# Output projections of four query tiles as two pairs, each in one PSUM bank with one sum of 512 columns, in the second and third slot of an attention round

## Chip, cores and metric

One core of a Trainium2 chip runs the whole program in one launch. The metric is the device time in microseconds (us), lower is better. In the profile PE is TensorE's matmuls, PEld its weight loads, DVE is VectorE, ACT is ScalarE, POOL is GpSimd and SP is SyncE.

## The reference

A layer norm is followed by attention and by a mixture of experts, whose result gates the attention's:

```python
xn = _layernorm(x, axis=-1)                       # x: (4, 512, 256)
q, k, v = xn @ Wq, xn @ Wk, xn @ Wv               # 16 query heads, 4 key/value heads of 128
q, k = rope_xpos(q), rope_xpos(k)
attn = softmax(where(causal, q @ k.T / sqrt(128), -inf))
s = (attn @ v).reshape(B, S, 2048) @ Wo           # the output projection: 2048 -> 256
g = _silu(moe(xn))                                # 16 experts, top 2, and a shared one
out = x + s * g
```

## The kernel before

Attention runs in 16 **rounds**. Round i handles group i: one batch of 512 tokens and one key/value head with its four query heads (j = 0 to 3). Every value of importance is kept as a pair of a high and a low half (fp16 and bf16), so each product is three matmuls (`PASSES`).

Five engines work on a round at the same time, each with its instructions in an order written out by hand (`round_`, once for each engine), and they meet only through semaphores that count upwards. For head h the stages are:

- TensorE `score` (L1465): scores of a head, three PSUM banks, 1280 columns in all.
- VectorE `row_max` (L1151) masks and takes the maximum; ScalarE `exponentials` (L809); VectorE `invert_sums` (L1157) gives 1/sum; GpSimd `divide` (L569) multiplies the probabilities by it.
- TensorE `transpose_probs` (L1478): ten transposes of the divided probabilities, in three units (0, 1) and (2); ScalarE copies the high half (L817), VectorE subtracts the low half (L1163).
- TensorE `weigh_values` (L1494): probabilities times values into bank 5; ScalarE `output_hi` (L831), VectorE `output_lo` (L1169).
- TensorE `project_out(rd, q)` (L1510): in round i the finished heads of round i - 1 are multiplied by Wo for query tile q, 4 heads x 3 passes = 12 matmuls of 256 columns; VectorE `add_projection` (L1176) adds the result to `s_sb` in SBUF.

In the same round the queries and the key of round i + 1 are prepared: TensorE `project` (L1434) of q0, q1, k, q2, q3, VectorE `rotate_products` (L1133, L1137, L1138), GpSimd `rotate_sum` (L556), ScalarE `rotate_hi` (L797), GpSimd `rotate_lo` (L563). Projections of all kinds are **items**: they use PSUM banks 6 and 7 in turn, in the order of a list. The item at place n waits until the item at place n - 2 has been read (`misc_free`). `project_values` (L1449, L1142) is the item v.

TensorE's order in a round of the loop, with `score(0')` for head 0 of the next round (T is `transpose_probs`, W is `weigh_values`):

| slot | order on TensorE |
|---|---|
| j = 0 | score(1), q0, T(0; 0, 1), W(last head of the round before), v, T(0; 2) |
| j = 1 | score(2), T(1; 0, 1), q1, **o0**, T(1; 2), W(0) |
| j = 2 | score(3), T(2; 0, 1), k, **o1**, T(2; 2), W(1) |
| end | q2, **o2**, T(3; 0, 1), W(2), score(0'), q3, T(3; 2), **o3** |

VectorE's order at the end of a round is `output_lo(1)`, the products of q2, `add_projection(2)`, the low halves of T(3; 0, 1), `row_max` of head 0', `output_lo(2)`, the first product of q3, `invert_sums` of head 0', the other products of q3, the low half of T(3; 2), `add_projection(3)`. GpSimd's is `divide` of head 3, the sum of k, the low halves of q1 and k, the sum of q2, an extra part (`ahead_of_division`), `divide` of head 0', the low half of q2.

The extra part differs between rounds. Rounds 6 to 13 scatter the rows of two token tiles to DRAM there and in the slots before (L598, L602); rounds 1 to 5 prepare weights and the routing of tokens to experts on GpSimd and VectorE; round 14 prepares shared weights (L587). Rounds 7 to 13 are a hardware loop, the others are unrolled. In round 0 there is no earlier output to project. Round 15 prepares no next round. After it, in the epilogue, o0 to o3 of the last group follow one another on TensorE, and then the expert part begins.

Of the kernel before, what the change touches and what calls it, by code (L numbers as in the profile page):

```python
# [18 lines left out]
P = 128  # L19
B, S, D = 4, 512, 256  # L20
# [54 lines left out]
ITEMS_FIRST = ["q0", "v", "x10", "q1", "x11", "x20", "k", "x21", "x30", "q2", "q3", "x31"]  # L75
ITEMS_LOGITS = ["q0", "v", "g0", "q1", "o0", "g1", "k", "o1", "g2", "q2", "o2", "q3", "o3", "g3"]
ITEMS_RANK = ["q0", "v", "rank", "q1", "o0", "k", "o1", "q2", "o2", "q3", "o3"]
ITEMS_TILE = ["q0", "v", "q1", "o0", "k", "o1", "q2", "o2", "q3", "o3", "tile"]
ITEMS_LOOP = ["q0", "v", "q1", "o0", "k", "o1", "q2", "o2", "q3", "o3"]
ITEMS_LAST = ["v", "o0", "o1", "o2", "o3"]  # L80
ITEMS_EPILOGUE = ["o0", "o1", "o2", "o3"]

# [120 lines left out]
def build(nc, x, wq, wk, wv, wo, gate_t, w_gate_up, w_down, shared_gu, shared_down, rope, ident, mask, iota, tri, rows, digits, out):  # L203
    with ExitStack() as ctx:
# [16 lines left out]
        s_sb = sb("s_sb", [P, NT * D], F32)  # L221
# [765 lines left out]
        def _(dve):  # L987
# [183 lines left out]

            def add_projection(rd, q):
                at = ((rd.i - 1) // NKV) * (QT * D) + q * D
                dve.wait_ge(misc_ps, rd.item(f"o{q}"))
                dve.wait_ge(misc_free, rd.item(f"o{q}") - 4)
                dve.tensor_tensor(s_sb[:, bass.ds(at, D)], misc_bank[rd.bank(f"o{q}")][:, 0:D], s_sb[:, bass.ds(at, D)],  # L1176
                                  ALU.add).then_inc(misc_free, 1)
# [61 lines left out]
            def round_(rd):  # L1239
# [11 lines left out]
                for j in range(GH - 1):  # L1251
# [5 lines left out]
                    if j == 0:  # L1257
                        if rd.first:
                            first_rope("q3", PROLOGUE.rot("q1"))
                            probs_lo(rd.head(j), j, (0, 1))  # L1260
                        routing(rd, 0)
                        rope("q0", (h, par))
                        if not rd.first:
                            probs_lo(rd.head(j), j, (0, 1))
                        if not rd.first:
                            output_lo(rd, -1)
                        value_lo(rd)
                    else:
# [99 lines left out]
        def _(pe):  # L1368
# [129 lines left out]

            def project_out(rd, q):
                i, item, ps = rd.i - 1, rd.item(f"o{q}"), misc_bank[rd.bank(f"o{q}")]  # L1500
# [5 lines left out]
                for j in range(GH):  # L1506
                    if rd is EPILOGUE and j == GH - 1:
                        pe.wait_ge(o_lo, rd.i * GH)
                    for n, (a, m) in enumerate(PASSES):
                        ins = pe.matmul(ps[:, 0:D], heads[a][:, j * S + q * P:j * S + (q + 1) * P], w[m][:, j * D:(j + 1) * D],  # L1510
                                        start=(j == 0 and n == 0), stop=(j == GH - 1 and n == 2))
                ins.then_inc(misc_ps, 1)
# [11 lines left out]
            def round_(rd):  # L1524
                queries = [rd.i * 5 + n for n in (1, PROLOGUE.rot("q1") if rd.first else 2, 4, 5)]
                for j in range(GH - 1):
# [12 lines left out]
                    else:  # L1539
# [180 lines left out]
```

## Time and profile before

| | |
|---|---|
| median of 3 runs | 711.22 us (711.12 to 712.67) |
| time of the profiled execution | 708.96 us |
| its span, first to last instruction | 707.1 us |
| busy: PE, DVE, ACT, POOL | 650.3, 566.1, 441.8, 549.8 us |
| granted TensorE clock, mean | 0.994 of full speed |
| instructions of `project_out` / `add_projection` | 768 matmuls / 64 sums |
| first and last sum into `s_sb` | 87.0 us and 554.1 us |

The page of a profile gives for each engine how long it was busy, and for each group of instructions its count, its mean duration and what ended the idle time before it. A row of a timeline merges neighbouring instructions of one kind: start, duration from the first start to the last end, count, and in square brackets the idle time before the first, with the engine and line that ended it. Matmuls overlap: the next begins before the last one's recorded end. Attention fills the stretch from about 20 to 554 us, the experts the rest.

### The profile page before, as it was taken

How to read it: one execution, taken by the hardware profiler on the slowest of the kernel's cores; microseconds unless marked ns; L12 is line 12 of the kernel's file. 1: busy time of each engine (PE TensorE's matmuls, PEld its weight loads, DVE VectorE, ACT ScalarE, POOL GpSimd, SP SyncE). 2: the span in 40 equal slices, each digit the busy share in tenths (PEclk: the TensorE clock that was granted, in tenths of full speed). 3: DMA queues.
4: the chain of work that ended last, by engine and by line, in shares of the span. 5: the costliest groups of instructions: out<-in, count | busy, mean ns of one | idle time of the engine just before them, and what ended most of it. 6: DMA issues, size and time to landing. Idle time of an engine off the chain costs nothing.

```text
span 707.1 us, 16044 instructions
## 1 busy us (share of the span) xinstructions
PE 650.3 (92%) x4928; PEld 458.2 (65%) x4993; DVE 566.1 (80%) x1660; ACT 441.8 (62%) x1203; POOL 549.8 (78%) x595
## 2 busy tenths in 40 slices
PE   3568899999999989999999999999998999999986
PEld 1245667666666656666666666666776777777753
DVE  5988999999999999998999999998985454333345
ACT  3577666676565756576766666576777765555532
POOL 4576878779788979898999899899898983555553
PEclk9999999999999999999999999999999999999997
DMA  9682000004100000000000000000043634677773
GB/s 296 194 270 84 1 1 3 1 1 110 45 1 1 8 8 24 23 7 22 15 15 15 15 15 22 22 7 24 2 65 91 188 90 96 144 147 148 228 259 130
DMA packets 64260, 50.28 MB, mean 71 GB/s; under 512 B 34704, under 2 KB 57584, under 8 KB 64208
## 3 DMA queue, kind: packets, MB, share of 16 engines
q1 hardware_dynamic: 60144, 39.19, 20.3%
q0 software_dynamic: 3792, 10.39, 4.9%
q8 instruction: 31, 0.51, 0.3%
q14 instruction: 21, 0.17, 0.1%
q10 hardware_dynamic: 272, 0.02, 0.0%
HBM read 24.73 MB, written 18.69 MB: 61 GB/s over the span
## 4 chain that ended last, share of the span: by engine, by line
PE 27%; POOL 26%; DVE 21%; issue 14%; ACT 7%; DMA 4%; SPq 0%; POOLq 0%; DVEq 0%; ACTq 0%
POOL arena L569 11%; PE bank L1621 8%; POOL arena L556 6%; PE bank L1655 6%; POOL arena L563 4%; DVE arena L1163 4%; ACT arena L809 4%; DVE arena L1138 3%; DVE arena L1137 3%; PE bank L1465 2%; POOL compare L598 2%; POOL xs_dram L602 2%; DVE arena L1133 2%; PE bank L1478 2%; PE bank L1630 2%
## 5 line engine op out<-in xcount | busy, mean ns | idle before, releaser
L569 POOL TENSOR_TENSOR arena<-arena,rinv 128x128 f32<-128x128 f32 (+3 forms) x256 | 176.2, 718 | 51.2 <-DVE rinv L1157 50.8
L809 ACT ACTIVATE arena<-bank,nmax 128x512 f32<-128x512 f32 (+3 forms) x256 | 132.5, 533 | 53.8 <-DVE nmax L1151 53.8
L1151 DVE CUSTOM_DVE_ANT_0 bank<-bank,mask_b 128x512 f32<-128x512 f32 (+3 forms) x256 | 118.0, 517 | 7.1 <-issue 7.0
L1434 PE MATMUL bank<-xnT_hi,arena 128*128 128x512 f16 (+1 forms) x320 | 110.2, 386 | 13.2 <-DVE arena L1138 7.2
L817 ACT CAST arena<-bank 128x512 f16<-128x512 f32 (+1 forms) x192 | 94.0, 526 | 43.6 <-PE bank L1478 42.7
L1465 PE MATMUL bank<-arena 128*128 128x384 f16 (+7 forms) x736 | 113.1, 296 | 4.6 <-POOL arena L563 2.7
L1494 PE MATMUL bank<-arena 128*128 128x512 bf16 (+2 forms) x765 | 114.7, 299 | 0.2
L1163 DVE TENSOR_TENSOR arena<-bank,arena 128x512 bf16<-128x512 f32 (+1 forms) x192 | 108.9, 595 | 4.2 <-ACT arena L817 3.1
L1478 PE MATMUL bank<-ident_f,arena 128*128 128x128 f32 x640 | 92.9, 276 | 13.3 <-DVE arena L1163 8.3
L556 POOL TENSOR_TENSOR arena<-arena 128x512 f32<-128x512 f32 x77 | 98.5, 1280 | 2.6 <-DVE arena L1138 2.6
L563 POOL TENSOR_TENSOR arena<-arena 128x512 bf16<-128x512 f32 x80 | 92.3, 1161 | 3.8 <-ACT arena L797 3.8
L1510 PE MATMUL bank<-arena 128*128 (+2 forms) x768 | 94.0, 273 | 0.4 <-DVE arena L1169 0.4
L1465 PEld LDWEIGHTS bank<-arena 128*128 128x128 f16 (+1 forms) x768 | 66.4, 98 | 41.1 <-issue 2.0
L1478 PEld LDWEIGHTS bank<-ident_f,arena 128*128 128x128 f32 x640 | 72.6, 141 | 29.3 <-DVE arena L1163 11.2
L1494 PEld LDWEIGHTS bank<-arena 128*128 128x128 f16 (+1 forms) x768 | 66.9, 98 | 36.9 <-DVE arena L1169 0.4
L1510 PEld LDWEIGHTS bank<-arena 128*128 (+2 forms) x768 | 75.1, 98 | 18.1 <-DVE arena L1169 0.7
L1346 DVE TENSOR_TENSOR arena<-bank,arena 128x176 f32<-128x176 f32 x79 | 27.0, 341 | 71.9 <-ACT arena L944 71.6
L733 POOL DMA_INDIRECT ys_dram<-arena,row_u x47 | 45.1, 960 | 50.5 <-ACT arena L955 50.5
L797 ACT CAST arena<-arena 128x512 f16<-128x512 f32 x80 | 50.5, 632 | 32.1 <-POOL arena L556 28.0
L1434 PEld LDWEIGHTS bank<-xnT_hi,arena 128*128 128x128 f16 (+1 forms) x320 | 31.6, 99 | 47.6 <-DVE arena L1138 9.2
L831 ACT CAST arena<-bank 128x512 f16<-128x512 f32 (+1 forms) x64 | 37.6, 587 | 36.6 <-PE bank L1494 36.1
L1133 DVE TENSOR_TENSOR arena<-bank,tab 128x512 f32<-128x512 f32 x80 | 54.7, 684 | 6.9 <-POOL arena L563 5.8
(149 smaller groups left out, 1174.1 us busy)
## 6 DMA issues: line engine op xcount, KB each, us to landing
stage<-w_gate_up SPq DMA_DIRECT2D x16, 352.0 KB
xs_dram<-s_sb SPq DMA_DIRECT2D x3, 1548.0 KB, 12.7
arena<-ys_dram SPq DMA_DIRECT2D x8, 512.0 KB, 7.7
stage<-w_down SPq DMA_DIRECT2D x16, 176.0 KB
stage<-wq SPq DMA_DIRECT2D x4, 512.0 KB, 8.7
stage<-wo SPq DMA_DIRECT2D x4, 512.0 KB, 7.4
stage<-x SPq DMA_DIRECT2D x1, 2048.0 KB, 11.2
out<-s_sb SPq DMA_DIRECT2D x8, 256.0 KB, 2.1
```

The source lines that it names most:

```text
L556: pool.tensor_tensor(rot_a[buf], rot_a[buf], rot_b[buf], ALU.add).then_inc(rot_add, 1)
L563: pool.tensor_tensor(dst, rot_a[buf], hi, ALU.subtract).then_inc(rot_lo, 1)
L569: ins = pool.tensor_tensor(pr, pr, rinv[:, par, qt:qt + 1].to_broadcast([P, (qt + 1) * P]), ALU.mult)
L809: ins = act.activation(probs[par][:, P_AT[qt]:P_AT[qt] + n], score_bank[u][:, col:col + n], ACT.Exp, scale=-1.0, bias=nmax[:, par, qt:qt + ...
L817: act.copy(pT[j % 2][0][:, at:at + cols], pt_bank[(3 * j + u) % 2][:, 0:cols]).then_inc(pt_hi, 1)
L1151: ins = dve.tensor_tensor_reduce(score_bank[u][:, col:col + n], score_bank[u][:, col:col + n], mask_b[:, S - n:S], -1.0, 3e38, ALU.add, AL ...
L1163: dve.tensor_tensor(pT[j % 2][1][:, at:at + cols], pt_bank[(3 * j + u) % 2][:, 0:cols], pT[j % 2][0][:, at:at + cols], ALU.subtract).then_ ...
L1434: ins = pe.matmul(ps[:], w[a][:, c * chunk:c * chunk + DH], tokens[m][:, c * TOK:c * TOK + S], start=(c == 0 and n == 0), stop=(c == KC - ...
L1465: ins = pe.matmul(score_bank[u][:, col:col + n_k], qT[a][:, j * S + qt * P:j * S + (qt + 1) * P], kT[m][:, 0:n_k], start=(n == 0), stop=(n ...
L1478: ins = pe.transpose(pt_bank[(3 * j + u) % 2][:, col + (qt - kt) * P:col + (qt - kt + 1) * P], probs[j % 2][:, P_AT[qt] + kt * P:P_AT[qt] ...
L1494: ins = pe.matmul(o_bank[:, kt * P:S], v_s[a][:, kt * DH:(kt + 1) * DH], pT[j % 2][m][:, PT_AT[kt]:PT_AT[kt] + n_q], start=(kt == 0 and n ...
L1510: ins = pe.matmul(ps[:, 0:D], heads[a][:, j * S + q * P:j * S + (q + 1) * P], w[m][:, j * D:(j + 1) * D], start=(j == 0 and n == 0), stop= ...
```

## The change

The four items o0 to o3 of a round become two, oa (query tiles 0 and 1) and ob (query tiles 2 and 3). Each writes both halves of its PSUM bank with 24 matmuls, and one VectorE sum of 512 columns reads the bank. oa stands where o0 stood, in slot j = 1, and ob where o1 stood, in slot j = 2. At the places of o2 and o3 nothing is left. The lists of items lose two entries each, and since an item waits for the one two places ahead of it, q3 waits for ob instead of q2, q0 of the next round for q2 instead of q3, and v for q3 instead of o3. Rounds 1 and 6 have extra items at the end of their lists (g3, the router's logits of the last batch, L1399, and tile, L1418): these waited for q3 and now wait for q2. VectorE's wait on `misc_free` ahead of a sum is dropped. The epilogue has oa and ob too. The matmuls themselves are the same ones, as many as before.

```diff
-ITEMS_LOOP = ["q0", "v", "q1", "o0", "k", "o1", "q2", "o2", "q3", "o3"]
-ITEMS_LAST = ["v", "o0", "o1", "o2", "o3"]
-ITEMS_EPILOGUE = ["o0", "o1", "o2", "o3"]
+ITEMS_LOOP = ["q0", "v", "q1", "oa", "k", "ob", "q2", "q3"]
+ITEMS_LAST = ["v", "oa", "ob"]
+ITEMS_EPILOGUE = ["oa", "ob"]
...
+OUT_PAIRS = {"oa": (0, 1), "ob": (2, 3)}
...
-            def add_projection(rd, q):
-                at = ((rd.i - 1) // NKV) * (QT * D) + q * D
-                dve.wait_ge(misc_ps, rd.item(f"o{q}"))
-                dve.wait_ge(misc_free, rd.item(f"o{q}") - 4)
-                dve.tensor_tensor(s_sb[:, bass.ds(at, D)], misc_bank[rd.bank(f"o{q}")][:, 0:D], s_sb[:, bass.ds(at, D)],
+            def add_projection(rd, name):
+                at = ((rd.i - 1) // NKV) * (QT * D) + OUT_PAIRS[name][0] * D
+                dve.wait_ge(misc_ps, rd.item(name))
+                dve.tensor_tensor(s_sb[:, bass.ds(at, 2 * D)], misc_bank[rd.bank(name)][:], s_sb[:, bass.ds(at, 2 * D)],
                                   ALU.add).then_inc(misc_free, 1)
...
                         if not rd.first:
-                            add_projection(rd, j - 1)
+                            add_projection(rd, ("oa", "ob")[j - 1])
...
                 rope("q2")
-                if not rd.first:
-                    add_projection(rd, 2)
                 probs_lo(rd.head(3), 3, (0, 1))
...
-                else:
-                    add_projection(rd, 3)
...
                         if not rd.first:
-                            project_out(rd, j - 1)
+                            project_out(rd, ("oa", "ob")[j - 1])
...
                 if not rd.last:
                     project(rd, "q2")
-                if not rd.first:
-                    project_out(rd, 2)
                 transpose_probs(rd.head(3), 3, (0, 1), rd.first)
...
-                else:
-                    project_out(rd, 3)
```

TensorE in slot j = 1 of round 3, from the last matmul of q1 (L1434) to the first of W(0) (L1494); T is L1478 and the output projection L1510. The lines of the changed kernel are one to three numbers off those of the kernel before. Before:

```order
L1434 MATMUL bank<-xnT_lo,arena 128x512
L1434 MATMUL bank<-xnT_hi,arena 128x512
L1510 MATMUL bank<-arena 128x256 x12
L1478 MATMUL bank<-ident_f,arena 128x128 x2
L1494 MATMUL bank<-arena 128x512 x3
```

and in the changed kernel:

```order
L1432 MATMUL bank<-xnT_lo,arena 128x512
L1432 MATMUL bank<-xnT_hi,arena 128x512
L1509 MATMUL bank<-arena 128x256 x24
L1476 MATMUL bank<-ident_f,arena 128x128 x2
L1492 MATMUL bank<-arena 128x512 x3
```

Twelve more matmuls stand ahead of T(1; 2) and W(0). Slot j = 2 changes in the same way, ahead of T(2; 2) and W(1).

TensorE at the end of round 3, from the last matmuls of W(1) over q2 to T(3; 0, 1). Before:

```order
L1494 MATMUL bank<-arena 128x256 x3
L1434 MATMUL bank<-xnT_hi,arena 128x512
L1434 MATMUL bank<-xnT_lo,arena 128x512
L1434 MATMUL bank<-xnT_hi,arena 128x512 x2
L1434 MATMUL bank<-xnT_lo,arena 128x512
L1434 MATMUL bank<-xnT_hi,arena 128x512
L1510 MATMUL bank<-arena 128x256 x12
L1478 MATMUL bank<-ident_f,arena 128x128 x8
```

and in the changed kernel:

```order
L1492 MATMUL bank<-arena 128x256 x3
L1432 MATMUL bank<-xnT_hi,arena 128x512
L1432 MATMUL bank<-xnT_lo,arena 128x512
L1432 MATMUL bank<-xnT_hi,arena 128x512 x2
L1432 MATMUL bank<-xnT_lo,arena 128x512
L1432 MATMUL bank<-xnT_hi,arena 128x512
L1476 MATMUL bank<-ident_f,arena 128x128 x8
```

The twelve matmuls of o2 no longer stand between q2 and T(3; 0, 1); by then 24 more than before have passed. The twelve of o3, after T(3; 2) at the end of the round, are gone likewise.

VectorE at the end of round 3, from the split of head 1's output (L1169) over the products of q2 (L1133, L1137, L1138) to the low halves of T(3; 0, 1) (L1163). Before:

```order
L1169 TENSOR_TENSOR arena<-bank,arena 128x512
L1133 TENSOR_TENSOR arena<-bank,tab 128x512
L1137 TENSOR_TENSOR arena<-bank,tab 64x512
L1138 TENSOR_TENSOR arena<-bank,tab 64x512
L1176 TENSOR_TENSOR s_sb<-bank,s_sb 128x256
L1163 TENSOR_TENSOR arena<-bank,arena 128x512 x2
```

and in the changed kernel:

```order
L1172 TENSOR_TENSOR arena<-bank,arena 128x512
L1136 TENSOR_TENSOR arena<-bank,tab 128x512
L1140 TENSOR_TENSOR arena<-bank,tab 64x512
L1141 TENSOR_TENSOR arena<-bank,tab 64x512
L1166 TENSOR_TENSOR arena<-bank,arena 128x512 x2
```

The sum of 256 columns behind the products of q2 is gone, as is the one at the end of the round.

## Rows read from the trace of the kernel before

**Rows 1.** Windows view of one loop round: busy us (x instructions) per engine

```profile
302.20:333.90 31.70, 31.00 (x235) 21.59 (x239) 28.96 (x85) 20.91 (x61) 28.90 (x33) 1.00 0.05 17
```

**Rows 2.** Timeline of VectorE: the split of the values in rounds 8 and 14

```profile
307.22 0.68 DVE L1142 TENSOR_TENSOR arena<-bank,arena 128x512 bf16<-128x512 f32 x1
...
497.41 0.68 DVE L1142 TENSOR_TENSOR arena<-bank,arena 128x512 bf16<-128x512 f32 x1
```

**Rows 3.** Timeline of TensorE, round 8: start, us, instructions [idle before <- releaser]

```profile
302.17 1.09 PE L1478 MATMUL bank<-ident_f,arena 128*128 128x128 f32 x8 [0.40 <-POOL arena L569]
...
310.24 1.47 PE L1510 MATMUL bank<-arena 128*128 x12
311.55 0.38 PE L1478 MATMUL bank<-ident_f,arena 128*128 128x128 f32 x2
...
318.98 1.79 PE L1494 MATMUL bank<-arena 128*128 128x512 f16 x12
...
321.89 0.38 PE L1434 MATMUL bank<-xnT_hi,arena 128*128 x1
322.11 1.47 PE L1510 MATMUL bank<-arena 128*128 x12
...
329.07 1.47 PE L1510 MATMUL bank<-arena 128*128 x12
...
333.89 0.98 PE L1478 MATMUL bank<-ident_f,arena 128*128 128x128 f32 x7 [0.42 <-POOL arena L569]
```

**Rows 4.** Timeline of GpSimd, the same round

```profile
319.34 2.74 POOL L569 TENSOR_TENSOR arena<-arena,rinv 128x128 f32<-128x128 f32 x4 [0.64 <-DVE rinv L1157]
...
325.52 1.25 POOL L556 TENSOR_TENSOR arena<-arena 128x512 f32<-128x512 f32 x1
...
331.01 2.74 POOL L569 TENSOR_TENSOR arena<-arena,rinv 128x128 f32<-128x128 f32 x4
```

**Rows 5.** Chain of waits over that round, by line

```profile
by line: POOL arena L569 31.0%; issue 25.8%; POOL arena L556 18.4%; POOL arena L563 15.9%; POOL compare L598 7.0%; POOL xs_dram L602 6.7%; POOLq L722 0.4%; POOLq L555 0.2%; POOLq L598 0.1%; POOLq L672 0.1%; POOLq L566 0.1%; POOLq L562 0.1%
```

**Rows 6.** Groups by line: the sum into s_sb, and a sum of 512 columns

```profile
L1176 DVE TENSOR_TENSOR s_sb<-bank,s_sb 128x256 f32<-128x256 f32 (+1 forms) x64 | 27.0, 422 | 4.6 <-PE bank L1510 3.2
...
L1142 DVE TENSOR_TENSOR arena<-bank,arena 128x512 bf16<-128x512 f32 x16 | 10.9, 683 | 0.3
```

**Rows 7.** Timeline of VectorE, the same round, from the split of head 1's output

```profile
321.75 0.69 DVE L1169 TENSOR_TENSOR arena<-bank,arena 128x512 f32 x1 [0.29 <-ACT arena L831]
322.40 0.69 DVE L1133 TENSOR_TENSOR arena<-bank,tab 128x512 f32<-128x512 f32 x1
...
323.81 0.68 DVE L1138 TENSOR_TENSOR arena<-bank,tab 64x512 f32<-64x512 f32 x1
324.53 0.43 DVE L1176 TENSOR_TENSOR s_sb<-bank,s_sb 128x256 f32 x1
```

**Rows 8.** Timeline of round 3: TensorE, then VectorE, then GpSimd

```profile
160.24 0.38 PE L1434 MATMUL bank<-xnT_hi,arena 128*128 128x512 f16 x1
...
171.65 1.04 PE L1478 MATMUL bank<-ident_f,arena 128*128 128x128 f32 x8
...
161.30 0.67 DVE L1133 TENSOR_TENSOR arena<-bank,tab 128x512 f32<-128x512 f32 x1
...
168.19 0.18 DVE L1157 RECIPROCAL rinv<-rsum 128x4 f32<-128x4 f32 x1
...
168.45 2.75 POOL L569 TENSOR_TENSOR arena<-arena,rinv 128x128 f32<-128x128 f32 x4 [0.30 <-DVE rinv L1157]
```

**Rows 9.** Timeline of TensorE: waits in rounds 1, 6 and 15

```profile
106.26 0.17 PE L1399 MATMUL bank<-gate_hi,xnT_hi 128*128 128x16 f16 x1 [1.05 <-DVE arena L1138]
...
267.62 0.16 PE L1418 MATMUL bank<-digit_b,tile_b 47*1 47x12 bf16 x1 [1.05 <-DVE arena L1138]
...
535.37 1.09 PE L1478 MATMUL bank<-ident_f,arena 128*128 128x128 f32 x8 [0.58 <-POOL arena L569]
```

**Rows 10.** Chain of waits in round 6: a stop of VectorE

```profile
247.78 3.33 DVE before L1114
```

More of the change, by code:

```diff
@@ L75 @@
 ITEMS_FIRST = ["q0", "v", "x10", "q1", "x11", "x20", "k", "x21", "x30", "q2", "q3", "x31"]
-ITEMS_LOGITS = ["q0", "v", "g0", "q1", "o0", "g1", "k", "o1", "g2", "q2", "o2", "q3", "o3", "g3"]
-ITEMS_RANK = ["q0", "v", "rank", "q1", "o0", "k", "o1", "q2", "o2", "q3", "o3"]
-ITEMS_TILE = ["q0", "v", "q1", "o0", "k", "o1", "q2", "o2", "q3", "o3", "tile"]
-ITEMS_LOOP = ["q0", "v", "q1", "o0", "k", "o1", "q2", "o2", "q3", "o3"]
-ITEMS_LAST = ["v", "o0", "o1", "o2", "o3"]
-ITEMS_EPILOGUE = ["o0", "o1", "o2", "o3"]
+ITEMS_LOGITS = ["q0", "v", "g0", "q1", "oa", "g1", "k", "ob", "g2", "q2", "q3", "g3"]
+ITEMS_RANK = ["q0", "v", "rank", "q1", "oa", "k", "ob", "q2", "q3"]
+ITEMS_TILE = ["q0", "v", "q1", "oa", "k", "ob", "q2", "q3", "tile"]
+ITEMS_LOOP = ["q0", "v", "q1", "oa", "k", "ob", "q2", "q3"]
+ITEMS_LAST = ["v", "oa", "ob"]
+ITEMS_EPILOGUE = ["oa", "ob"]
 X_AT = [["x10"], ["x11", "x20"], ["x21", "x30"], ["x31"]]
@@ L87 @@
 assert 2 * (LATE - SCATTER_FROM) == NT
+OUT_PAIRS = {"oa": (0, 1), "ob": (2, 3)}
+assert 2 * D * 4 == 2048
 ROT = ["q0", "q1", "k", "q2", "q3"]
@@ L1310, in _ @@
             output_lo(EPILOGUE, -1)
-            for q in range(QT):
-                add_projection(EPILOGUE, q)
+            for name in OUT_PAIRS:
+                add_projection(EPILOGUE, name)
             def add_shared(g):
@@ L1496, in weigh_values, with project_out @@
                 ins.then_inc(pv, 1)
-            def project_out(rd, q):
-                i, item, ps = rd.i - 1, rd.item(f"o{q}"), misc_bank[rd.bank(f"o{q}")]
+            def project_out(rd, name):
+                i, item, ps = rd.i - 1, rd.item(name), misc_bank[rd.bank(name)]
                 pe.wait_ge(o_lo, rd.i * GH - 1 if rd is EPILOGUE else rd.i * GH)
@@ L1505, in project_out @@
                 w = [t[:, bass.ds((i % NKV) * (GH * D), GH * D)] for t in wo_s]
[L1506 to L1511, printed above, removed]
+                for c, q in enumerate(OUT_PAIRS[name]):
+                    for j in range(GH):
+                        if rd is EPILOGUE and name == "oa" and c == 0 and j == GH - 1:
+                            pe.wait_ge(o_lo, rd.i * GH)
+                        for n, (a, m) in enumerate(PASSES):
+                            ins = pe.matmul(ps[:, c * D:(c + 1) * D], heads[a][:, j * S + q * P:j * S + (q + 1) * P], w[m][:, j * D:(j + 1) * D],
+                                            start=(j == 0 and n == 0), stop=(j == GH - 1 and n == 2))
                 ins.then_inc(misc_ps, 1)
@@ L1580, in _ @@
             weigh_values(EPILOGUE, -1)
-            for q in range(QT):
-                project_out(EPILOGUE, q)
+            for name in OUT_PAIRS:
+                project_out(EPILOGUE, name)
             experts = [None]
```

## Prediction

> **What bounds the kernel now.** I looked first at the busy shares of one round of the loop in the windows view, to see which engine is full. TensorE is busy 31.00 of 31.70 us, VectorE 28.96, GpSimd 28.90, ScalarE 20.91 [rows 1]. No single engine is far ahead, so the busy shares can't say what a shifted instruction costs; the handovers must. The period is constant: the split of the values comes at 307.22 in round 8 and at 497.41 in round 14, so six rounds take 190.19 us, 31.70 each [rows 2].
>
> Then I read the timeline of TensorE for round 8 [rows 3]. The round's turning point is the transposing of head 0, T(0; 0, 1): it starts at 302.17 after 0.40 us of idle time that GpSimd's division ended, and the next one, at 333.89, after 0.42 us that the same line ended. From 302.17 to the end of q2 TensorE hardly stops. GpSimd ends the round with a stretch that has no slack: from the sum of q2 at 325.52 to the division of head 0' at 331.01, which lasts 2.74 us and releases the transposing at 333.89 [rows 3, 4]. The chain of waits over this round is made of GpSimd's lines alone, with 25.8% called issue [rows 5]. But it hides a second path of nearly equal length: TensorE from T(0; 0, 1) to q2, then VectorE's products of q2, then GpSimd's sum of q2 and what is behind it. The engines run in a ring, and the ring is what I price.
>
> **What the change does to engines' own work.** TensorE has the same matmuls. Twelve of them take 311.55 - 310.24 = 1.31 us of its time [rows 3]. VectorE loses 64 sums of 422 ns and gains 32 of 512 columns. The trace has no such sum with two fp32 inputs; the split of the values, also 512 columns out of PSUM, takes 683 ns [rows 6]. From below the price can't be less than one small sum, 422 ns, from above not more than two, 844; I take 683, the nearest row. That frees 2 x 422 - 683 = 161 ns a pair, 5.2 us over 32 pairs. It would show in the time only where VectorE is the bound throughout.
>
> The Trainium skill, "VectorE: DVE Perf Modes", section "The TRN2 errata", says that each Vector instruction pays a fixed price, 120 cycles of 0.96 GHz for one that reads PSUM, and advises operands of 512 elements and more. By its figures a pair would save 125 ns, 4.0 us in all (an estimate from that page). The rows say 161 ns, so they agree in kind; neither tells whether the saved time is on the path.
>
> **What the moves cost in a round of the loop.** Follow the ring from T(0; 0, 1):
>
> 1. oa adds 12 matmuls ahead of T(1; 2), W(0) and score(3): +1.31 us. ob adds 12 more ahead of W(1) and q2. So the end of W(1) and of q2 come 2 x 1.31 = 2.62 us later, counted from T(0; 0, 1). Nothing on TensorE hides this, since it hardly stops there.
> 2. Behind q2, VectorE's first product starts at 322.40; the last matmul of q2 ended at 321.89 + 0.38 = 322.27, and W(1), by way of ScalarE and the split of head 1's output (321.75), is ready at the same time [rows 3, 7]. No slack here: the products start about 2.6 us later. A wait of 0.29 us of VectorE for ScalarE stands ahead of them and only grows. The product chain ends at 323.81 + 0.68 = 324.49 [rows 7].
> 3. GpSimd starts the sum of q2 at 325.52 [rows 4]. A handover takes about 0.1, so the slack is 325.52 - 324.49 - 0.1 = 0.93 us. GpSimd's own queue comes later too: its division of head 3 already waits 0.64 us for VectorE's inverse [rows 4], which hangs on W(0) and so moves by 1.31. That is less than what arrives through q2, so it is covered by it.
> 4. From the sum of q2 to the next T(0; 0, 1) it takes 333.89 - 325.52 = 8.37 us of GpSimd's work, unchanged.
>
> The ring becomes longer by 2.62 - 0.93 = 1.69, I take **1.65 us** because the split path (2) has some hundredths of play. What o2 and o3 give back, 2.62 us on TensorE between q2 and the next T(0; 0, 1), is worth nothing: TensorE reaches that transposing earlier and waits for the division. Its idle time there should grow from 0.42 to about 2. Queued behind that waiting transposing are W of the last head, v and score(2), so all of the round moves. Seven rounds (7 to 13): 7 x 1.65 = 11.55 us.
>
> **The other rounds.** In rounds 2 to 5 and 14 GpSimd has less to do and VectorE carries the ring. In round 3 q2 ends at 160.24 + 0.38 = 160.62, VectorE starts on it at 161.30, so beyond a handover of 0.13 the slack is 0.55. From there VectorE works through to the inverse at 168.19, without o2's sum from now on (-0.42). GpSimd divides from 168.45 for 2.75 us, to 171.20, and T follows at 171.65: the usual handover is 0.14 (331.01 + 2.74 to 333.89), so 0.31 is slack [rows 3, 4, 8]. The round grows by 2.62 - 0.55 - 0.42 - 0.31 = 1.34 us. Rounds 2, 4, 5 and 14 have the same order with other small parts between; the least is 0, the most 2.62 - 0.42 = 2.20; I take 1.5, near round 3. Together 1.34 + 4 x 1.5 = 7.3 us.
>
> Rounds 1 and 6 lose a wait: TensorE stands 1.05 us for q3's products ahead of the logits in round 1, and as long ahead of the tile item in round 6 [rows 9], and both items now ask for q2 only. In round 6 VectorE also stops for 3.33 us [rows 10] just ahead of the split of head 0's output, which covers the later W(0). I take 0 for each, between -1.05 and +1.3. In round 15 oa comes 1.31 us ahead of score(3), against an idle time of 0.58 us at T(2; 0, 1) [rows 9] and some at T(1; 2): I take 0.2, between 0 and 0.73. In the epilogue the 48 matmuls follow one another as before, and the last VectorE sum is 0.26 us longer; the expert part on TensorE doesn't ask for it.
>
> **The sum.** 11.55 + 7.3 + 0.2 = 19.05 us. On the profiled execution (708.96 us, span 707.1) that is 728.0; it stands 2.26 below the median of the runs, 711.22, so the median should be 711.22 + 19.05 = **730.3 us**.
>
> **The rivals.**
>
> - *Faster, VectorE's time decides.* If the stretches in which VectorE is the fullest engine set the end and the later q2 were absorbed, the 5.2 us of saved sums would show: 711.2 - 5.2 = 706. For it: in the early rounds VectorE goes from 161.30 to 168.19 without a stop [rows 8]. Against it: TensorE's shift in a round is 2.62 us, the saving 0.32. It decides only if the slack behind q2 were above 2.3 us, and it is 0.93 and 0.55.
> - *No change, TensorE decides.* TensorE is the fullest engine [rows 1], its matmuls are the same, and the waits ahead of T(0; 0, 1) are only 0.4 us [rows 3]. If its own work sets the period, moving it within a round is free: 711. It would need the division of head 0' to be ready early, and GpSimd's rows show it as the one that releases [rows 3, 4]. The Trainium skill, "Perfetto Trace Analysis", section "Identifying the Most-Contended Engine", says to look for the engine with the highest occupancy and to improve that one; by that rule nothing that counts changes here, and the time would be this rival's.
> - *Slower by half.* If GpSimd or ScalarE has room that I don't see, and only oa's 1.31 us count, by way of W(0) and the inverse of head 3 (which GpSimd already waits for), less the 0.42 of VectorE in rounds with a VectorE ring: 7 x 1.31 + 5 x 0.6 = 12.2, 723.4.
> - *Slower by all.* If the slack is used up otherwise, since VectorE and GpSimd come later too, rounds 1 to 14 pay up to the full 2.62: 14 x 2.62 = 36.7, 748; with half of the slack, 739.
>
> **How the numbers follow.** My forecast, 724 to 737, has a chance of 0.74; slower by half 0.10; slower by more 0.06; no change 0.04; faster 0.04; the rest in between. The range that leaves out 2 in 10 is 722 to 738: its lower end takes in the loop's share alone (711.2 + 11.55 = 722.8) and rounds 2 to 5 and 14 at nothing, its upper end all of them at 2.2 and the loop at 2.2 (711.2 + 12 x 2.2 = 737.6). A measurement of this kernel tells a change from none at about 0.2%, 1.4 us; faster than that has 0.04, within it 0.04, slower 0.92.
>
> **What would show it.** In the changed profile: (1) the period of the loop's rounds at 33.3 to 33.4 us; (2) idle time of TensorE ahead of T(0; 0, 1), ended by GpSimd's division, of about 2 us in place of 0.4; (3) in the loop, VectorE's split of head 1's output about 22.2 us after T(0; 0, 1), where it was 321.75 - 302.17 = 19.58; (4) GpSimd waiting for VectorE's last product of q2, where it waited for nothing; (5) its wait for the inverse of head 3 about as long or longer than 0.64; (6) 32 sums of 512 columns at about 0.68 us. It would be wrong if the period stayed at 31.7, above all if GpSimd's sum of q2 were not waited for, or if T(0; 0, 1) came without a wait.

## The result and the profile after

The changed kernel takes 732.86 us (median of 5 runs, 728.49 to 734.53), the kernel before 711.12 beside it (5 runs, 710.73 to 712.67): ratio 1.0305, 95% interval 1.0279 to 1.0331. It is slower by 3%, 21.7 us. The profiled execution took 728.49 us, with a span of 726.7; it is the shortest of the five, with a mean granted clock of 0.986 where the other four have 0.976 to 0.978.

TensorE over one turn of the ring in rounds 8 and 9, timeline as in [rows 3] (L1476 is T, L1509 oa or ob, L1492 W, L1463 scores, L1432 a projection):

```profile
306.58 1.97 PE L1476 MATMUL bank<-ident_f,arena 128*128 128x128 f32 x8 [2.13 <-POOL arena L572]
...
341.04 1.09 PE L1476 MATMUL bank<-ident_f,arena 128*128 128x128 f32 x8 [2.13 <-POOL arena L572]
...
349.11 2.78 PE L1509 MATMUL bank<-arena 128*128 x24
351.73 0.38 PE L1476 MATMUL bank<-ident_f,arena 128*128 128x128 f32 x2
...
353.58 1.79 PE L1463 MATMUL bank<-arena 128*128 128x512 f16 x12
355.21 1.04 PE L1476 MATMUL bank<-ident_f,arena 128*128 128x128 f32 x8
...
357.38 2.78 PE L1509 MATMUL bank<-arena 128*128 x24
...
360.22 1.79 PE L1492 MATMUL bank<-arena 128*128 128x512 f16 x11
361.85 0.38 PE L1432 MATMUL bank<-xnT_hi,arena 128*128 x1
...
362.93 0.38 PE L1432 MATMUL bank<-xnT_hi,arena 128*128 x1
```

The next T(0; 0, 1) starts at 374.05, so this turn takes 33.01 us where it was 31.72 [rows 3]; TensorE rests 2.13 us ahead of it, where it rested 0.40. The turn before it took 341.04 - 306.58 = 34.46, and its first eight transposes took 1.97 us in place of 1.09.

VectorE (the wait that grew, with the products of q2 behind it; as [rows 7]) and its groups, whose last numbers are idle time and its releaser (as [rows 6]):

```profile
360.63 0.69 DVE L1178 TENSOR_TENSOR s_sb<-bank,s_sb 128x512 f32 x1
...
362.90 0.69 DVE L1172 TENSOR_TENSOR arena<-bank,arena 128x512 f32 x1 [1.25 <-ACT arena L834]
363.51 0.68 DVE L1136 TENSOR_TENSOR arena<-bank,tab 128x512 f32<-128x512 f32 x1
...
364.91 0.69 DVE L1141 TENSOR_TENSOR arena<-bank,tab 64x512 f32<-64x512 f32 x1
...
L1178 DVE TENSOR_TENSOR s_sb<-bank,s_sb 128x512 f32<-128x512 f32 (+1 forms) x32 | 22.1, 690 | 4.7 <-PE bank L1509 3.8
```

GpSimd in the same turn (as [rows 4]): the division of head 3, the sum of q2, the division of head 0':

```profile
359.27 2.74 POOL L572 TENSOR_TENSOR arena<-arena,rinv 128x128 f32<-128x128 f32 x4 [1.72 <-DVE rinv L1160]
...
365.68 1.26 POOL L559 TENSOR_TENSOR arena<-arena 128x512 f32<-128x512 f32 x1 [0.20 <-DVE arena L1141]
...
371.17 2.74 POOL L572 TENSOR_TENSOR arena<-arena,rinv 128x128 f32<-128x128 f32 x4
```

GpSimd waits 1.72 us for the inverse of head 3 (was 0.64) and 0.20 for q2's last product (was none). From the sum of q2 to the next T(0; 0, 1) it takes 374.05 - 365.68 = 8.37 us, to the hundredth what it was. So the turn is longer by GpSimd's two waits: 1.72 + 0.20 - 0.64 = 1.28 of the 1.29 between these two turns.

The windows view of this turn (as [rows 1]: busy time by engine PE, PEld, DVE, ACT, POOL, then the granted clock) and of two microseconds each at the start of the next turn but not of this one:

```profile
340.80:373.90 33.10, 30.67 (x234) 21.64 (x238) 28.61 (x82) 21.14 (x61) 29.02 (x34) 1.00 0.04 16
...
341.00:343.00 2.00, 1.96 (x14) 1.47 (x15) 0.91 (x3) 1.87 (x8) 2.00 (x2) 1.00 0.00 0
...
372.00:374.00 2.00, 0.00 (x0) 0.00 (x0) 1.79 (x10) 1.33 (x4) 2.00 (x4) 1.00 0.03 8
374.00:376.00 2.00, 1.95 (x10) 1.38 (x11) 0.90 (x3) 1.96 (x8) 2.00 (x2) 0.69 0.00 0
376.00:378.00 2.00, 2.00 (x10) 1.12 (x9) 1.96 (x4) 0.63 (x2) 2.00 (x5) 0.50 0.00 0
378.00:380.00 2.00, 2.00 (x30) 1.86 (x29) 1.05 (x2) 0.77 (x2) 2.00 (x2) 0.96 0.00 0
```

Here is what the prediction had not thought of. TensorE rests until 374.05, and then the granted clock falls to 0.50, the 1.2 GHz level, and the matmuls take longer until about 378. It does so after five of the loop's rests, near 307, 375, 409, 443 and 511, and not after those at 341 and 477, which were as long (2.13 us). Each such turn takes about 34.4 us, 1.4 more. In the kernel before the windows of this stretch all have a granted clock of 1.00.

From one split of the values to the next, rounds 7 to 13 together take 238.25 us in place of 221.84: +16.4. Rounds 2 to 5 and 14 take 1.25, 1.02, 0.82, 0.80 and 1.37 more, 5.3 together. Round 1 takes 0.1 more and round 6 takes 0.5 less. What lies ahead of the first of these splits and behind the last (round 15, the epilogue and the experts) takes 1.6 less. Together 19.6, the growth of the span.

### The profile page after: what moved, and what is told of

Read it like the earlier page. It is cut to its first block, busy times and chain, and to the rows that moved or that the text cites. A ratio compares the mean times of both kernels' runs of the same rounds, so it can differ in the third digit from the quotient of the medians.

```text
span 726.7 us, 15889 instructions
## 1 busy us (share of the span) xinstructions
PE 653.9 (90%) x4928; PEld 461.1 (63%) x4993; DVE 564.5 (78%) x1628; ACT 444.4 (61%) x1203; POOL 550.3 (76%) x595
## 4 chain that ended last, share of the span: by engine, by line
PE 39%; POOL 22%; DVE 17%; issue 14%; ACT 6%; DMA 1%; POOLq 0%; SPq 0%; DVEq 0%; ACTq 0%
POOL arena L572 9%; PE bank L1616 9%; PE bank L1650 6%; PE bank L1492 5%; PE bank L1509 5%; POOL arena L566 4%; PE bank L1476 4%; POOL arena L559 4%; PE bank L1463 3%; PE bank L1432 3%; DVE arena L1166 3%; DVE arena L1141 3%; DVE arena L1140 3%; POOL xs_dram L605 3%; ACT arena L812 2%
## 5 line engine op out<-in xcount | busy, mean ns | idle before, releaser
L1476 PE MATMUL bank<-ident_f,arena 128*128 128x128 f32 x640 | 95.2, 281 | 29.3 <-POOL arena L572 23.4
L1492 PE MATMUL bank<-arena 128*128 128x512 f16 (+6 forms) x739 | 118.9, 306 | 2.7 <-DVE arena L1172 1.2
L1432 PE MATMUL bank<-xnT_hi,arena 128*128 128x512 f16 (+1 forms) x320 | 110.0, 385 | 10.2 <-DVE arena L1141 6.8
L1463 PE MATMUL bank<-arena 128*128 128x128 f16 (+7 forms) x748 | 114.4, 297 | 5.0 <-POOL arena L566 3.4
L1166 DVE TENSOR_TENSOR arena<-bank,arena 128x512 bf16<-128x512 f32 (+1 forms) x192 | 109.1, 596 | 4.9 <-ACT arena L820 3.4
L1476 PEld LDWEIGHTS bank<-ident_f,arena 128*128 128x128 f32 x640 | 75.2, 144 | 46.2 <-issue 17.0
L1492 PEld LDWEIGHTS bank<-arena 128*128 128x128 f16 (+1 forms) x768 | 69.1, 101 | 41.9 <-issue 5.8
L1463 PEld LDWEIGHTS bank<-arena 128*128 128x128 f16 (+1 forms) x768 | 64.9, 98 | 44.8 <-ACT arena L812 4.2
L1509 PE MATMUL bank<-arena 128*128 (+2 forms) x768 | 89.1, 273 | 0.4 <-DVE arena L1172 0.4
L1509 PEld LDWEIGHTS bank<-arena 128*128 (+2 forms) x768 | 75.1, 98 | 15.3 <-DVE arena L1172 0.7
L1172 DVE TENSOR_TENSOR arena<-bank,arena 128x512 bf16<-128x512 f32 (+1 forms) x64 | 44.0, 688 | 37.4 <-ACT arena L834 37.4
```

The costliest lines, as they stand in the source:

```text
L1166: dve.tensor_tensor(pT[j % 2][1][:, at:at + cols], pt_bank[(3 * j + u) % 2][:, 0:cols], pT[j % 2][0][:, at:at + cols], ALU.subtract).then_ ...
L1432: ins = pe.matmul(ps[:], w[a][:, c * chunk:c * chunk + DH], tokens[m][:, c * TOK:c * TOK + S], start=(c == 0 and n == 0), stop=(c == KC - ...
L1463: ins = pe.matmul(score_bank[u][:, col:col + n_k], qT[a][:, j * S + qt * P:j * S + (qt + 1) * P], kT[m][:, 0:n_k], start=(n == 0), stop=(n ...
L1476: ins = pe.transpose(pt_bank[(3 * j + u) % 2][:, col + (qt - kt) * P:col + (qt - kt + 1) * P], probs[j % 2][:, P_AT[qt] + kt * P:P_AT[qt] ...
L1492: ins = pe.matmul(o_bank[:, kt * P:S], v_s[a][:, kt * DH:(kt + 1) * DH], pT[j % 2][m][:, PT_AT[kt]:PT_AT[kt] + n_q], start=(kt == 0 and n ...
L1509: ins = pe.matmul(ps[:, c * D:(c + 1) * D], heads[a][:, j * S + q * P:j * S + (q + 1) * P], w[m][:, j * D:(j + 1) * D], start=(j == 0 and ...
```

## The experiments

Two questions: is the place of the 24 matmuls the cause, or the sharing of a bank and a sum; and which way around the ring carries the delay. The first four runs stood beside a kernel before of 710.88 us, the next three of 713.06, the last two of 710.31; ratios are each to their own.

**Half of the matmuls at the changed places.**

```diff
                         for n, (a, m) in enumerate(PASSES):
+                            if rd is not EPILOGUE and j % 2 == 1:
+                                continue
```

> The changed kernel, with 12 of the 24 matmuls of each output item left out in rounds 1 to 15 (heads 1 and 3 don't enter the output projection there). Items, banks, waits and the sums of 512 columns are those of the changed kernel; only TensorE's time ahead of W(0), W(1) and q2 is back to what it was before. Place theory: the ring from T(0; 0, 1) over q2, its products, the sum of q2 and the division is as long as before, so the loop's rounds take about 31.7 us, and the whole 706 to 712 us. TensorE will stand idle for some 3 us a round ahead of T(0; 0, 1); if that makes the granted clock fall, as it does in the changed kernel's profile, single rounds are up to 1.2 us longer, 717 at most. Sharing theory (the shared bank, the long sum or the changed waits cost the time): nothing of it is undone, 728 to 733.

Measured: 710.32 us, ratio 0.9999 (0.9982 to 1.0017). With 12 matmuls in each place in rounds 1 to 15, a turn takes 31.6 to 31.7 us; the whole loss is gone, though two query tiles still share a bank and a sum. But half of the projection's work is left out too, so this run doesn't tell the place of the matmuls from their number. The clock also fell after three of the rests (near 331, 396, 461), and those rounds took 33.0 us. They don't show in the total, since the loop's rounds 7 to 13 together take 4.2 us more than before, and rounds 1 to 6 and 14 take 4.3 less (round 1 alone 2.1). The first of the falls, with a window ahead of it and one behind:

```profile
328.00:330.00 2.00, 0.34 (x2) 0.00 (x0) 1.92 (x12) 1.20 (x3) 2.00 (x3) 1.00 0.15 52
330.00:332.00 2.00, 1.70 (x10) 1.36 (x11) 0.69 (x2) 1.79 (x8) 2.00 (x3) 0.72 0.00 0
332.00:334.00 2.00, 2.00 (x9) 0.92 (x8) 1.92 (x4) 0.98 (x2) 2.00 (x4) 0.50 0.00 0
```

**Two sums of 256 columns in place of the one of 512.**

```diff
-                dve.tensor_tensor(s_sb[:, bass.ds(at, 2 * D)], misc_bank[rd.bank(name)][:], s_sb[:, bass.ds(at, 2 * D)],
-                                  ALU.add).then_inc(misc_free, 1)
+                for c in range(2):
+                    ins = dve.tensor_tensor(s_sb[:, bass.ds(at + c * D, D)], misc_bank[rd.bank(name)][:, c * D:(c + 1) * D],
+                                            s_sb[:, bass.ds(at + c * D, D)], ALU.add)
+                ins.then_inc(misc_free, 1)
```

> The changed kernel, but VectorE reads each shared bank with two sums of 256 columns in place of one of 512. Place theory: VectorE waits for ScalarE ahead of both splits of the outputs anyway (1.45 and 1.25 us in the loop), which hides 0.1 to 0.2 us each: 732 to 734, the same as the changed kernel within the noise of its runs. If the long sum were what costs, this would go back towards 711.

Measured: 731.18 us, ratio 1.0302 (1.0273 to 1.0332), the same as the changed kernel's 1.0305 (the time is just under the 732 to 734 expected). The form of the sum is worth nothing that can be seen.

**Sharing without the move.** oa's halves at the old places of o0 and o1, ob's at those of o2 and o3:

```diff
-                            project_out(rd, j - 1)
+                            project_out(rd, "oa", (j - 1,))
...
                 if not rd.first:
-                    project_out(rd, 2)
+                    project_out(rd, "ob", (0,))
...
                 else:
-                    project_out(rd, 3)
+                    project_out(rd, "ob", (1,))
```

> The sharing without the move: query tiles 0 and 1 share a bank and a sum of 512 columns, 2 and 3 another, but the 12 matmuls of each stand where they stood before (slots j = 1, j = 2, behind q2, behind T(3; 2)). The bank stays open from the first half to the second; q0, q1, k, q2, q3 all use the other bank. The sums come in slot j = 2 and at the end of the round. Place theory: 710 to 712, no more than the 161 ns a pair of VectorE's time to be gained. Sharing theory: 725 or more.

Measured: 712.76 us, ratio 1.0036 (1.0017 to 1.0055), just above the 710 to 712 expected. The loop's rounds take 31.69 us and TensorE rests for 0.40 ahead of T(0; 0, 1), both as before. The 2.5 us arise in unrolled rounds (round 6 takes 1.05 more, round 1 0.5). Sharing costs no more than that, and the saved sums give nothing back: this is the direct answer to the place-or-sharing question. Whether the 2.5 us come from the sharing stays open, since the banks were dealt out anew for this run as well: v, oa and ob use one of them, and all projections of queries and keys the other.

**oa in slot j = 2, ob at the end.** The list of items shows the places; the calls move with it:

```diff
-ITEMS_LOOP = ["q0", "v", "q1", "oa", "k", "ob", "q2", "q3"]
+ITEMS_LOOP = ["q0", "v", "q1", "k", "oa", "q2", "q3", "ob"]
```

> Pairs as in the changed kernel, whole items of 24 matmuls, but oa in slot j = 2 and ob at the end of the round behind T(3; 2), where o3 stood. From T(0; 0, 1) to q2 there are 24 matmuls of output projection as before, from T(0; 0, 1) to W(0) 12 fewer. Place theory: the ring over q2 is as before, the inverse of head 3 comes 1.31 us earlier, so GpSimd's wait of 0.64 us for it goes; the loop's rounds take about 31.1 us, TensorE isn't idle for more than 0.5 us ahead of T(0; 0, 1), the clock holds, and the time is 706 to 709, under the kernel before. Sharing theory: 725 or more.

Measured: 711.76 us, ratio 1.0023 (1.0005 to 1.0041). A miss: the rounds take 31.93 us. Counted from T(0; 0, 1), score(3) starts after 10.11 us where it was 11.22, so TensorE reaches T(2; 0, 1) 1.1 us earlier and gains nothing; it waits there for the division of head 2. First its row, then two of GpSimd:

```profile
315.58 1.09 PE L1478 MATMUL bank<-ident_f,arena 128*128 128x128 f32 x8 [0.85 <-POOL arena L572]
```

```profile
319.70 2.75 POOL L572 TENSOR_TENSOR arena<-arena,rinv 128x128 f32<-128x128 f32 x4 [0.66 <-DVE rinv L1160]
...
326.10 1.26 POOL L559 TENSOR_TENSOR arena<-arena 128x512 f32<-128x512 f32 x1 [0.19 <-DVE arena L1141]
```

So the ring has an anchor that I had overlooked. T(2; 0, 1) can't be earlier than GpSimd's division of head 2, and in the kernel before it was already held by it. There the division ends at 312.43 + 2.74 = 315.17, and T(2; 0, 1) starts at 315.22 (its row is further down). GpSimd's row of before:

```profile
312.43 2.74 POOL L569 TENSOR_TENSOR arena<-arena,rinv 128x128 f32<-128x128 f32 x4
```

GpSimd's wait for the inverse of head 3 stays at 0.66: what it waits for was not TensorE's slot 1. The 24 matmuls now lie between T(2; 0, 1) and q2, where 12 lay, and q2 comes late by a little.

**The changed kernel with TensorE kept busy.** Ahead of T(0; 0, 1) of rounds 7 to 15:

```diff
+                    if u == 0 and j == 0 and (not isinstance(h, int) or h >= LATE * GH):
+                        pe.wait_ge(pt_lo, h * 3 - 1)
+                        for _ in range(BUSY):
+                            pe.matmul(pt_bank[0][:, 0:P], ident_b[:], ident_b[:], start=True, stop=True)
                     if u == 0:
                         pe.wait_ge(normed, h + 1)
```

> The changed kernel, with 30 extra matmuls of 128 columns on TensorE ahead of T(0; 0, 1) in rounds 7 to 15, into a bank that the transposes then overwrite. They depend on nothing but the bank, and fill most of the 2.1 us in which TensorE waits for GpSimd's division there. The output is not changed. Idle theory (TensorE's stop of 2.1 us is what makes the granted clock fall to half in some rounds, and that costs the ring 1.2 us each time): no round of the loop at a granted clock under 1.0, all of them at 33.2 us, so five times 1.2 us less than the changed kernel's profile: 725 to 728. If the clock falls for another reason, or the fall costs nothing: 730 to 734, or more, since TensorE does more work.

Measured: 728.57 us, ratio 1.0217 (1.0199 to 1.0235), against 1.0305 without them; the time is half a microsecond above the 725 to 728 expected. More work on TensorE made it faster than the changed kernel. In the two profiled executions rounds 7 to 13 take 231.35 us in place of 238.25, 6.9 less, though the spans differ by only 1.2: the prologue, round 0 and what lies behind the loop came out longer in this one, which isn't explained. Its timeline, and the windows of two of the stretches of 33 us, all of which have a clock of 1.00:

```profile
341.16 1.84 PE L1474 MATMUL bank<-ident_b 128*128 128x128 bf16 x30
343.37 1.09 PE L1481 MATMUL bank<-ident_f,arena 128*128 128x128 f32 x8 [0.38 <-POOL arena L573]
```

```profile
337.00:370.00 33.00, 32.61 (x270) 23.38 (x268) 28.59 (x83) 21.02 (x60) 28.94 (x33) 1.00 0.04 16
370.00:403.00 33.00, 32.61 (x270) 23.39 (x268) 28.59 (x83) 21.02 (x60) 28.95 (x33) 1.00 0.04 16
```

Rounds 8 to 13 take 33.0 us each and round 7 takes 33.2. This is the ring's own length without the clock: 33.01 - 31.68 = +1.33 a round. The falls cost the rest.

**oa in slot j = 1, ob at the end.**

```diff
-ITEMS_LOOP = ["q0", "v", "q1", "oa", "k", "ob", "q2", "q3"]
+ITEMS_LOOP = ["q0", "v", "q1", "oa", "k", "q2", "q3", "ob"]
```

> oa in slot j = 1 as in the changed kernel, ob at the end of the round behind T(3; 2). From T(0; 0, 1) to q2 there are 24 matmuls of output projection as before, but 24 of them stand ahead of W(0) and of T(2; 0, 1) in place of 12. The kernel before has T(2; 0, 1) just behind the division that it waits for, so 1.31 us more put it about 1.1 us later, and with it ScalarE's copies, the exponentials, the inverse of head 3 and GpSimd's division of head 3, behind which GpSimd has no slack. Expected: the loop's rounds at 32.8 us, 7 x 1.1 = 7.7 us there, some 3 us in the others: 719 to 724. If only the way over q2 counts, as my prediction's sum had it: 711.

Measured: 730.53 us, ratio 1.0232 (1.0210 to 1.0253), outside the 719 to 724 expected; rounds of 33.06 us, 0.26 above what I expected, and the unrolled ones longer too (round 3 by 2.1). GpSimd, from the division of head 3 to the division of head 0', and TensorE's T(0; 0, 1) behind it:

```profile
328.87 2.74 POOL L572 TENSOR_TENSOR arena<-arena,rinv 128x128 f32<-128x128 f32 x4 [2.02 <-DVE rinv L1160]
331.58 1.27 POOL L559 TENSOR_TENSOR arena<-arena 128x512 f32<-128x512 f32 x1
...
335.04 1.25 POOL L559 TENSOR_TENSOR arena<-arena 128x512 f32<-128x512 f32 x1
...
340.52 2.74 POOL L572 TENSOR_TENSOR arena<-arena,rinv 128x128 f32<-128x128 f32 x4
...
343.90 1.04 PE L1478 MATMUL bank<-ident_f,arena 128*128 128x128 f32 x8
```

The sum of q2 waits for nothing, and yet the round grows by 1.38, which is just what the wait for the inverse of head 3 grew by (2.02 - 0.64). oa in slot 1 with ob at the end lengthens the ring as much as the whole change, with nothing added ahead of q2. Not all of it is oa's: T(0; 0, 1) starts 343.90 - 343.26 = 0.64 behind the division of head 0', where 0.14 is usual, so with ob's 24 matmuls at the end TensorE now comes 0.50 late there. The run with ob in the same place and oa in slot 2 has rounds of 31.93, so oa's step from slot 2 to slot 1 costs about 33.06 - 31.93 = 1.13; in the changed kernel, where T(0; 0, 1) isn't late, the same wait grew by 1.72 - 0.64 = 1.08.

**oa behind q2, ob at the end.**

```diff
-ITEMS_LOOP = ["q0", "v", "q1", "oa", "k", "ob", "q2", "q3"]
+ITEMS_LOOP = ["q0", "v", "q1", "k", "q2", "oa", "q3", "ob"]
```

> oa behind q2 where o2 stood, ob at the end of the round. Nothing of the output projection stands between T(0; 0, 1) and q2 any more, 2.62 us less than before. Ring theory: GpSimd's ring (division of head 2, T(2; 0, 1), copies, exponentials, inverse, division of head 3, and so on to the next round) is untouched at 31.7 us a round, so this gains nothing in the loop; in rounds 2 to 5, where VectorE carries the ring from q2 on, TensorE's own 30.5 us and VectorE are the bound: 707 to 712. If TensorE's way to q2 still had a price, it would be clearly under 707.

Measured: 722.97 us, ratio 1.0142 (1.0120 to 1.0163), where 707 to 712 was expected; rounds of 32.55, a second miss. With nothing in slots 1 and 2, the ring isn't shorter, and 24 matmuls (12 before) now stand ahead of T(3; 0, 1), W(2) and score(0'), and 48 (24 before) between q2 and T(0; 0, 1). VectorE's stop ahead of the masking of those scores, GpSimd's division of head 2, its divisions of head 0' and head 1, and T(0; 0, 1):

```profile
331.20 0.69 DVE L1154 CUSTOM_DVE_ANT_0 bank<-bank,mask_b 128x512 f32<-128x512 f32 x1 [0.82 <-issue]
...
316.25 2.75 POOL L572 TENSOR_TENSOR arena<-arena,rinv 128x128 f32<-128x128 f32 x4 [0.35 <-DVE rinv L1160]
...
334.85 2.75 POOL L572 TENSOR_TENSOR arena<-arena,rinv 128x128 f32<-128x128 f32 x4
...
340.39 2.76 POOL L572 TENSOR_TENSOR arena<-arena,rinv 128x128 f32<-128x128 f32 x4 [0.44 <-DVE rinv L1160]
...
339.03 1.04 PE L1480 MATMUL bank<-ident_f,arena 128*128 128x128 f32 x8
```

VectorE's stop is hardly new: it was 0.63 in the kernel before. The rows of GpSimd say more. It waits 0.35 and 0.44 us for the inverses of heads 2 and 1, where it waited for neither, which is 0.79 of the 0.87 by which the round grew. And T(0; 0, 1) comes 339.03 - 337.60 = 1.43 behind the division of head 0', 1.29 later than the usual 0.14. So what stands behind q2 isn't free either: when TensorE comes late at T(0; 0, 1), the heads behind it come late. This is read from the rows; no run tested it.

**12 matmuls in slot 1, 36 in slot 2.** Is the way over q2 enough by itself? The products of tile 3 are written and then overwritten by those of tile 2, so tile 3's part of the projection is left out; TensorE's work stays whole.

```diff
-OUT_PAIRS = {"oa": (0, 1), "ob": (2, 3)}
+OUT_PAIRS = {'oa': ((0, 0),), 'ob': ((1, 3), (0, 1), (1, 2))}
...
-                for c, q in enumerate(OUT_PAIRS[name]):
+                for c, q in OUT_PAIRS[name]:
```

> One query tile's 12 matmuls stand in slot j = 1, as in the kernel before, and 36 in slot j = 2. TensorE's work is that of the changed kernel; the products of tile 3 are written and then overwritten by those of tile 2, so its part of the projection is left out of the sum. Score(3), T(1; 2) and W(0) come where they came in the kernel before, W(1) and q2 where they come in the changed kernel. Theory one, the way over q2 lengthens the ring by itself: q2 comes 2.62 later less some 0.45 of small stops of TensorE that vanish, and has 0.93 of slack: loop rounds of 32.9 to 33.1 us, GpSimd waits for q2's last product by about 1.2, its wait for the inverse of head 3 is short; time 722 to 731. Theory two, only the way over score(3) and the inverse of head 3 counts (24 matmuls in slot 1, as the run with oa in slot 1 and ob at the end suggests): loop rounds of 31.7 to 32.0, time 711 to 716.

Measured: 733.0 us, ratio 1.0298 (1.0262 to 1.0333), above both ranges; the clock fell in four of the loop's seven rounds (34.4 to 34.6 us), and the three in which it held take 33.2 us (33.24 in round 7), 0.14 above theory one's 33.1. GpSimd's two waits:

```profile
359.68 2.74 POOL L572 TENSOR_TENSOR arena<-arena,rinv 128x128 f32<-128x128 f32 x4 [0.66 <-DVE rinv L1160]
...
367.40 1.26 POOL L559 TENSOR_TENSOR arena<-arena 128x512 f32<-128x512 f32 x1 [1.20 <-DVE arena L1141]
```

The wait for the inverse is as before, that for q2's last product is 1.20. Theory two (only the way over score(3)) would have given 31.7 to 32.0, and is refuted as the only way.

**12 matmuls in slot 1, 24 in slot 2, TensorE kept busy** as above, the fourth tile left out:

```diff
+OUT_PAIRS = {'oa': ((0, 0),), 'ob': ((0, 1), (1, 2))}
```

> 12 matmuls (tile 0) in slot j = 1 and 24 (tiles 1 and 2) in slot j = 2; tile 3's products and its part of the sum are left out, 12 matmuls of a round. 30 matmuls of 128 columns on constants stand ahead of T(0; 0, 1) in rounds 7 to 15, so that TensorE doesn't rest there. Against the kernel before only W(1) and q2 come later, by 1.31 us less what vanishes of small stops (0 to 0.45), so by 0.9 to 1.3, against a slack of 0.93. Theory one (the way over q2 with this slack): loop rounds of 31.7 to 32.1. Theory two (that way has more slack): 31.7 or less. If rounds take over 32.3, the slack behind q2 was misread. Time 708 to 715.

Measured: 709.03 us, ratio 0.9971 (0.9949 to 0.9993), for three quarters of the output projection; rounds of 31.93 us, inside theory one's 31.7 to 32.1:

```profile
324.07 1.26 POOL L560 TENSOR_TENSOR arena<-arena 128x512 f32<-128x512 f32 x1 [0.20 <-DVE arena L1142]
```

It is the round of the run with oa in slot 2: same length, same wait of 0.2, since both have 24 matmuls between T(2; 0, 1) and q2 and a T(2; 0, 1) held by the division.

No placement of whole pairs beat the kernel before.

## Why the prediction came out as it did

The forecast was 730.3 and the result 732.86, inside 722 to 738. The mechanism was right, but the nearness of the number comes in part from two errors of opposite sign.

**The ring (term of 11.55 us).** Six signs were named. TensorE's rest ahead of T(0; 0, 1) is 2.13 us, as forecast; GpSimd waits for q2's last product (0.20) and longer for the inverse of head 3 (1.72); the 32 sums take 690 ns for 683. Two are off by the same bit: the split of head 1's output comes 362.90 - 341.04 = 21.86 after T(0; 0, 1) for 22.2, and the turn takes 33.0 for 33.3 to 33.4. The failing step is the first: "Nothing on TensorE hides this, since it hardly stops there". It did stop, twice, too briefly for a bracket. Timeline of TensorE before, round 8: score(3), T(2; 0, 1), and q2 behind W(1), which starts at 318.98 [rows 3]:

```profile
313.39 1.79 PE L1465 MATMUL bank<-arena 128*128 128x512 f16 x11
315.22 1.09 PE L1478 MATMUL bank<-ident_f,arena 128*128 128x128 f32 x8
...
320.81 1.03 PE L1434 MATMUL bank<-xnT_hi,arena 128*128 x3
```

From score(3) to T(2; 0, 1) it takes 1.83, and from W(1) to q2 1.83: the one held by GpSimd's division of head 2 (to 315.17), the other by VectorE's last product of k, which frees q2's bank (319.98 + 0.68 = 320.66). In the changed kernel 355.21 - 353.58 = 1.63 and 361.85 - 360.22 = 1.63. Each was a stop of 0.20 that the later arrival used up: 2.62 - 0.40 = 2.22, less the slack of 0.93 makes 1.29. Measured 1.33, where I took 1.65. The same account fits the other runs, with x for the 1.31 us of twelve matmuls: 36 in slot 2 use only the second stop, 2x - 0.20 - 0.93 = 1.49 (measured 33.24 - 31.68 = 1.56); 24 between a held T(2; 0, 1) and q2 give x - 0.20 - 0.93 = 0.18 (measured 0.25, twice). Seven rounds at 1.33 are 9.3 us. The run with oa in slot 1 and ob at the end (1.38) and the one with both behind q2 (0.87) don't go by this account, since there T(0; 0, 1) itself comes late.

**The clock (no term at all).** 16.4 - 9.3 = 7.1 us of the loop's growth is left, and five falls at 34.46 - 33.01 = 1.45 are 7.25. The run with TensorE kept busy has no fall in the loop and no such rounds, so this part is shown, not argued. The prediction named the 2 us rest and called it free: "TensorE reaches that transposing earlier and waits for the division". The rest itself was free; what followed it in five of seven cases wasn't.

**GpSimd's other wait.** Step 3 said that the division of head 3 waits for an inverse "which hangs on W(0)", covered by what arrives through q2. For the changed kernel the sum came out, since q2 is still 0.20 later. But it is hardly a lesser path: the wait for this inverse grew by 1.08 in the changed kernel, against 1.28 in all, and the run with oa in slot 1 and nothing added ahead of q2 gave +1.38. And a slot 1 without matmuls did not shorten the wait of 0.66. That fits a start held by GpSimd's own division of head 2, whose T(2; 0, 1) ScalarE must copy before the next exponentials; this last link I read from the order of the rows and did not test.

**The rounds outside the loop.** 5.3 us for the 7.3 taken: round 3 was worked out at 1.34 and grew by 1.02, and taking the others "near round 3" put them too high; rounds 4 and 5 grew by 0.8. Rounds 1 and 6 were taken at 0 and came to +0.1 and -0.5. The 1.6 us gained outside the rounds aren't explained, nor is it known which part holds the 2 us by which the medians differ more (21.7) than the profiled spans (19.6). Both kernels have a stretch at a clock of 0.5 near the end, before from about 689 and again near 706, after from about 723; no run tested what it does to the time.

**The rivals.** *No change*, with the rule of the most contended engine behind it ("Perfetto Trace Analysis" in the Trainium skill, section "Identifying the Most-Contended Engine"), falls: TensorE is the fullest engine in both kernels, its matmuls are the same, and the time grew by 3%; the run with 30 more matmuls a round took less time than the changed kernel. The prediction used that rule short of its exception: the same section of the Trainium skill says that the busy share of matmuls is no good measure of how close TensorE is to its limit, and names that of its weight loads instead. By these (21.59 of 31.70 us [rows 1]) VectorE and GpSimd come first, one with less work after the change and the other with the same, so the rule would still not have given a loss. *Faster by VectorE* falls with the run with two sums: the Trainium skill's advice on operands of 512 elements ("VectorE: DVE Perf Modes", section "The TRN2 errata") agrees with the duration of a sum (690 ns for 844), and the time doesn't show it. *Slower by half* had a real mechanism, the way over score(3) and head 3, but not as the only one: 36 matmuls in slot 2 leave it alone and lose as much. Its time, 723.4, was missed by 9.5 us.

## What to carry to other kernels

In a kernel whose engines hand work around a ring, price a move by the matmuls that come to lie between two handovers, and read each gap as start minus start of neighbouring rows: stops of 0.2 us show in no bracket of the matmul rows, and two of them, 0.40 us, are what the forecast of a round lacked (1.65, measured 1.33). Look for anchors as well, work that another engine releases at a fixed time, since moving TensorE's work away from ahead of them gained nothing here. And where a change makes TensorE rest, ask whether its clock holds.

## What the runs showed of the hardware

Rests of TensorE of 2.05 to 2.13 us were followed by a granted clock of 0.50 (the 1.2 GHz level) in five of the loop's seven turns, and by 1.00 in the other two. Rests of 1.95 and 1.96 us in the half-matmul run were too, in three of its seven turns; rests of 0.40 us (the kernel before) and 0.75 us (oa in slot 1, ob at the end) were followed by no fall in the loop. With 30 matmuls of 128 columns in the rest (1.84 us of it busy), no fall came in the loop. In the half-matmul run too a round with a fall took 33.02 us and one without about 31.65. The Trainium skill, "TensorE: Matmul & The Clock Gate", section "Part 1: The HAM clock gate", says that a clock gate halves the array's clock, by how busy TensorE has been. The rows agree, with 0.50 from 376 us on, after a window without one matmul; what sets apart the rests that kept the clock stays open here.
